# The first tile table of an attention and expert kernel: its running sum as a masked product and one sum, its parts dealt over other sequences

## What is computed

```python
x = x + attention(layernorm(x), ctx, ctx)        # 16 heads of 16 features
probs = softmax(layernorm(x) @ router)           # 8 experts
weights, picks = top_k(probs, 2)                 # two experts for each token
x = x + sum_over_the_two_picks(weight * down[e](silu(h @ gating[e]) * (h @ up[e])))
```

## Time and profile before

| | |
|---|---|
| median of 3 runs | 1268.08 us |
| lowest, highest | 1267.72, 1269.12 us |
| the profiled execution | 1269.64 us, its span 1267.9 us |
| TensorE busy | 1221.0 us (96% of the span) |
| VectorE busy | 646.1 us (51%) |
| ScalarE busy | 562.0 us (44%) |
| POOL busy | 423.9 us (33%) |
| mean granted TensorE clock | 0.993 of full |
| stage A | 0 to about 533 us |
| expert stage | about 533 us to the end |

### The profile page before, as it was taken

How to read it: one execution, slowest core, us unless ns; L and a number is a source line. 1 busy time by engine, 2 the same in 40 slices (tenths; PEclk the granted TensorE clock), 3 DMA queues, 4 the chain that set the end, 5 groups by cost and what they waited for, 6 DMA issues and landing times.

```text
span 1267.9 us, 30811 instructions
## 1 busy us (share of the span) xinstructions
PE 1221.0 (96%) x11246; PEld 994.7 (78%) x11247; DVE 646.1 (51%) x1762; ACT 562.0 (44%) x926; POOL 423.9 (33%) x354
## 2 busy tenths in 40 slices
PE   7999999999999999689999999999999999999996
PEld 5677677777767766578887888888888888888996
DVE  3778787888888878623453333222222222332332
ACT  4566666666666665525322222222222222222442
POOL 4112333333333333322563222333332322222322
PEclk9999999999999999889999999999999999999999
DMA  5444444455544432414444333333333333333432
GB/s 150 135 118 127 148 148 147 152 151 154 151 138 151 122 114 82 113 38 68 80 90 68 52 52 51 53 50 50 51 52 50 52 53 51 50 51 42 54 51 32
DMA packets 171586, 112.45 MB, mean 89 GB/s; under 512 B 103344, under 2 KB 158640, under 8 KB 171472
## 3 DMA queue, kind: packets, MB, share of 16 engines
q1 hardware_dynamic: 143984, 72.75, 23.5%
q0 software_dynamic: 26400, 37.09, 16.8%
q10 hardware_dynamic: 1088, 1.05, 0.2%
HBM read 48.59 MB, written 45.46 MB: 74 GB/s over the span
## 4 chain that ended last, share of the span: by engine, by line
PE 87%; DVE 5%; DMA 2%; issue 2%; another core or an unknown queue 2%; ACT 1%; SPq 0%; POOL 0%; ACTq 0%; POOLq 0%; DVEq 0%
PE banks L527 69%; PE banks L556 5%; PE banks L570 5%; PE banks L581 4%; DVE row_max L1064 1%; PE banks L562 1%; PE banks L533 1%; DMA heads<-qT 1%; PE banks L597 1%; DMA out<-x_sb,token 1%; PE banks L605 1%; DVE att_rows L1077 1%; DVE q_less L1071 1%; DMA x_sb<-in_x 0%
## 5 line engine op out<-in xcount | busy, mean ns | idle before, releaser
L486 POOL DMA_INDIRECT out<-x_sb,token x135 | 210.3, 1558 | 477.1 <-DVE x_sb L1386 409.9
L895 ACT ACTIVATE qT<-banks 128x1024 f32<-128x1024 f32 (+1 forms) x75 | 70.3, 938 | 473.7 <-PE banks L527 412.5
L1380 DVE TENSOR_TENSOR heads<-qT,banks 128x1024 f32<-128x1024 f32 (+1 forms) x75 | 83.5, 1114 | 355.8 <-PE banks L527 340.2
L527 PE MATMUL banks<-xnT,probs 128*128 128x256 f32 (+1 forms) x1184 | 242.5, 362 | 4.8 <-issue 4.8
L527 PE MATMUL banks<-down_sb,heads 128*128 x1080 | 245.5, 379 | 1.6 <-DVE x_sb L1386 0.9
L527 PE MATMUL banks<-xnT,kT 128*128 128x256 f32 (+1 forms) x1216 | 242.9, 357 | 3.6 <-ACT probs L889 3.6
L527 PEld LDWEIGHTS banks<-xnT,probs 128*128 128x128 f32 x1184 | 209.2, 191 | 33.2 <-issue 7.7
L527 PEld LDWEIGHTS banks<-xnT,kT 128*128 128x128 f32 x1216 | 211.7, 190 | 29.4 <-issue 4.3
L527 PEld LDWEIGHTS banks<-down_sb,heads 128*128 128x128 f32 x1080 | 204.0, 190 | 29.2 <-issue 2.2
L439 POOL DMA_INDIRECT sorted_x<-xn,slots_now x128 | 124.9, 976 | 251.1 <-PE banks L556 140.9
L1064 DVE TENSOR_REDUCE row_max<-banks 128x16 f32<-128x2048 f32 x64 | 146.6, 2291 | 58.6 <-PE banks L556 58.4
(11 more groups left out here) (168 smaller groups left out, 1293.0 us busy)
## 6 DMA issues: line engine op xcount, KB each, us to landing
xn<-sorted_x SPq DMA_DIRECT2D x240, 64.0 KB
x_sb<-in_x SPq DMA_DIRECT2D x16, 512.0 KB, 3.9
ctxT_sb<-in_ctx SPq DMA_DIRECT2D x16, 512.0 KB
heads<-kT SPq DMA_DIRECT2D x128, 64.0 KB
heads<-qT SPq DMA_DIRECT2D x128, 64.0 KB
out<-x SPq DMA_DIRECT2D x16, 512.0 KB
gate_sb<-_L_ffn_kernel_gating_EDF SPq DMA_DIRECT2D x8, 512.0 KB
up_sb<-in_L_ffn_kernel_up_EDF SPq DMA_DIRECT2D x8, 512.0 KB
```

The costliest lines, as they stand in the source:

```text
L486: pool.indirect_dma_start(out=out[:, :], out_offset=bass.IndirectOffsetOnAxis(ap=token[:, v, h:h + 1], axis=0), in_=ys[:, 2 * u + h, :], i ...
L527: last = nc.tensor.matmul(dst, lhsT, rhs, start=(i == 0), stop=(i == len(pairs) - 1))
L895: nc.scalar.activation(gatedT[:, 0:w * F], gate_up[:, 0:w * F], ACT.Silu).then_inc(s_silu, 1)
L1380: nc.vector.tensor_tensor(fusedT[:, u, 0:w * F], gatedT[:, 0:w * F], gate_up[:, 1024:1024 + w * F], ALU.mult).then_inc(s_fuse, 1)
```

## The change

The running sum over the experts becomes a product of `n_pairs` with a constant mask of 8 by 8 ones and zeroes (`up_to`, one where the second expert is not after the first) and one sum over the last axis. POOL makes the mask once, near its start. Every `add_up_tiles` of the early and the late table uses this form. The notes `done_to` and `done` move from the early table to the start of part 1 of the late table. The early table's parts are dealt anew: the counting and the running sum behind sequence 59, the expert of each tile and the tiles skipped behind sequence 60, the writing of the tables behind sequence 61. Step counts change with it (24 to 15 for the early table).

```diff
+        up_to = sb("up_to", [P, EXPERTS, EXPERTS])
...
-        EARLY_STEPS = 24
+        EARLY_STEPS = 15
         PADS_MADE = EARLY_STEPS + 3
-        PAIR_STEPS = EARLY_STEPS + 32
-        TABLE_STEPS = PAIR_STEPS + 24
+        PAIR_STEPS = EARLY_STEPS + 29
+        TABLE_STEPS = PAIR_STEPS + 18
...
             root(1)
+            nc.gpsimd.memset(up_to[:], 1.0).then_inc(s_up_to, 1)
+            pool.wait_ge(s_up_to, 1)
+            nc.gpsimd.affine_select(out=up_to[:], in_=up_to[:], compare_op=ALU.is_ge, fill=0.0, base=0,
+                                    pattern=[[1, EXPERTS], [-1, EXPERTS]], channel_multiplier=0).then_inc(s_up_to, 1)
             for i in range(SPARE_TILES):
                 pool.dma_start(sorted_x[SPARE + i * P:SPARE + (i + 1) * P, :], blank[:]).then_inc(s_blank, 16)
...
-            def add_up_tiles(steps, experts):
-                if experts[0] == 1:
-                    steps.then(nc.vector.tensor_copy(tiles_to[:], n_pairs[:]))
-                for e in experts:
-                    steps.then(nc.vector.tensor_tensor(tiles_to[:, e:e + 1], tiles_to[:, e - 1:e], n_pairs[:, e:e + 1], ALU.add))
+            def add_up_tiles(steps, room):
+                part = room[:, 0:EXPERTS * EXPERTS].rearrange("p (a b) -> p a b", b=EXPERTS)
+                steps.then(nc.vector.tensor_tensor(part, n_pairs[:].unsqueeze(1).broadcast_to([P, EXPERTS, EXPERTS]), up_to[:],
+                                                   ALU.mult))
+                steps.then(nc.vector.reduce_sum(tiles_to[:], part, AX.X))
...
                 if part == 1:
                     tile_starts_passed(steps, over)
                     steps.then(nc.vector.reduce_sum(n_pairs[:], over[:, :, 0:m:2], AX.X))
+                    add_up_tiles(steps, early_rooms[1])
                 if part == 2:
-                    add_up_tiles(steps, range(1, 5))
+                    experts_of_tiles(steps, past, EARLY)
+                    tiles_skipped(steps, past, past_tiles, n_pairs, EARLY)
                 if part == 3:
-                    add_up_tiles(steps, range(5, EXPERTS))
-                    steps.then(nc.vector.tensor_scalar(done_to[:], tiles_to[:], float(EARLY), None, ALU.min))
-                    steps.then(nc.vector.tensor_tensor(done[:, 1:EXPERTS], done_to[:, 1:EXPERTS], done_to[:, 0:EXPERTS - 1],
-                                                       ALU.subtract))
-                    steps.then(nc.vector.tensor_copy(done[:, 0:1], done_to[:, 0:1]))
-                if part == 4:
-                    experts_of_tiles(steps, past, EARLY)
-                if part == 5:
-                    tiles_skipped(steps, past, past_tiles, n_pairs, EARLY)
                     write_table(steps, 0, EARLY, 2 * P)
...
             def late_table(part):
...
                 if part == 1:
                     steps = Steps(dve, s_table, EARLY_STEPS, 6)
+                    steps.then(nc.vector.tensor_scalar(done_to[:], tiles_to[:], float(EARLY), None, ALU.min))
+                    steps.then(nc.vector.tensor_tensor(done[:, 1:EXPERTS], done_to[:, 1:EXPERTS], done_to[:, 0:EXPERTS - 1],
+                                                       ALU.subtract))
+                    steps.then(nc.vector.tensor_copy(done[:, 0:1], done_to[:, 0:1]))
                     steps.then(nc.vector.tensor_tensor(n_pairs[:], n_pairs[:], done[:, 0:EXPERTS], ALU.subtract))
-                    add_up_tiles(steps, range(1, EXPERTS))
+                    add_up_tiles(steps, late_rooms[1])
...
                 if part == 3:
-                    add_up_tiles(steps, range(1, EXPERTS))
+                    add_up_tiles(steps, late_rooms[1])
...
                     if b == 3 and g == EARLY_GROUPS + 2:
                         early_table(1)
+                    if b == 0 and g == EARLY_GROUPS + 3:
                         early_table(2)
+                    if b == 1 and g == EARLY_GROUPS + 3:
                         early_table(3)
-                    if b == 0 and g == EARLY_GROUPS + 3:
-                        early_table(4)
-                    if b == 1 and g == EARLY_GROUPS + 3:
-                        early_table(5)
```

More of the change, by code:

```diff
@@ L198, in moe_attention @@
         s_qh = [sem("query_heads_spread_0"), sem("query_heads_spread_1")]
-        s_res, s_blank, s_pad = (sem(n) for n in ("resid_stored", "blanks_written", "pads_written"))
+        s_res, s_blank, s_pad, s_up_to = (sem(n) for n in ("resid_stored", "blanks_written", "pads_written", "prefix_mask_ready"))
         s_rows_out = [sem(f"rows_written_room{r}") for r in range(ROOMS)]
@@ L1213, in early_table @@
                     steps.then(nc.vector.reduce_sum(n_pairs[:], over[:, :, 0:m:2], AX.X))
+                    add_up_tiles(steps, early_rooms[1])
                 if part == 2:
-                    steps = Steps(dve, s_table, 0, 3)
-                    add_up_tiles(steps, range(1, 5))
+                    steps = Steps(dve, s_table, 0, 5)
+                    experts_of_tiles(steps, past, EARLY)
+                    tiles_skipped(steps, past, past_tiles, n_pairs, EARLY)
                 if part == 3:
-                    steps = Steps(dve, s_table, 0, 8)
-                    add_up_tiles(steps, range(5, EXPERTS))
-                    steps.then(nc.vector.tensor_scalar(done_to[:], tiles_to[:], float(EARLY), None, ALU.min))
-                    steps.then(nc.vector.tensor_tensor(done[:, 1:EXPERTS], done_to[:, 1:EXPERTS], done_to[:, 0:EXPERTS - 1],
-                                                       ALU.subtract))
-                    steps.then(nc.vector.tensor_copy(done[:, 0:1], done_to[:, 0:1]))
-                if part == 4:
-                    steps = Steps(dve, s_table, 0, 14)
-                    experts_of_tiles(steps, past, EARLY)
-                if part == 5:
-                    steps = Steps(dve, s_table, 0, 16)
-                    tiles_skipped(steps, past, past_tiles, n_pairs, EARLY)
+                    steps = Steps(dve, s_table, 0, 10)
                     write_table(steps, 0, EARLY, 2 * P)
@@ L1258, in late_table @@
                 if part == 2:
-                    steps = Steps(dve, s_table, EARLY_STEPS, 20)
+                    steps = Steps(dve, s_table, EARLY_STEPS, 17)
                     experts_of_tiles(steps, past, LATE)
@@ L1273, in late_table @@
                     past, past_tiles, over = table_room(late_rooms, SINGLES)
-                    steps = Steps(dve, s_table, PAIR_STEPS, 12)
+                    steps = Steps(dve, s_table, PAIR_STEPS, 6)
                     experts_of_tiles(steps, past, SINGLES)
```

## The result

The changed kernel took 1265.16 us in the median of 6 runs (1262.54 to 1267.68), the kernel before 1269.26 us in the median of 6 (1267.72 to 1270.0). The ratio is 0.9967, with a 95% interval of 0.9952 to 0.9981: 4.1 us faster, and clear of no change. The profiled execution took 1262.54 us, with a span of 1260.8.

A forecast was written before the change was run, and what follows sets the result against it. TensorE was taken as the bound, except where it waited for VectorE's row maxima of sequences 60 and 62. Terms -1.64 + 0.46 - 0.86 = -2.04 us gave 1266.0 us from the 1268.08 median; range 1263.0 to 1268.9.

The forecast's parts named there:

- the likeliest case: Whole kernel: the measured time would lie within 0.2% (2.5 us) of no change; chance 0.52.
- Part 1: Behind sequence 59: shorter sum and moved notes free VectorE 1.68 us earlier; TensorE's idle time limits the gain to -1.64 us.
- Part 2: Behind sequence 60: the `tiles_skipped` steps arrive, delaying the maximum of 61 up to 0.86 us; +0.46 us shows.
- Part 3: Behind sequence 61: the `tiles_skipped` steps leave the path to the maximum of 62; all counts, -0.86 us.
- rival A: The forecast itself: all three terms, both half-clock stretches (518 to 526, 546 to 554) as before; 1266.0 us, chance 0.50.
- the sign of A: In the granted-clock windows after the change, two stretches below 1.0 would show that the forecast's own case held.
- Rival B: Less idle time keeps TensorE's clock up: first stretch gone, -3.9 us, 1264.2; second too, 1262.4; chance 0.24.
- Rival C: Gain given back at VectorE's wait before 545.23, if that ends by a clock of its own; 1268.1 us, chance 0.14.
- the unnamed wait: VectorE's 12.45 us wait before the last attention's turning at 545.23, for something the profile does not name.
- Rival D: Slower: 0.46 us more TensorE waiting behind sequence 60 brings the clock down there; 1269.4 us, chance 0.12.
- third stretch: Another half-clock stretch, behind sequence 60, like that of 518 to 526 (8 us at 0.57), costing 3.4 us.
- The covers: Late table hidden beside TensorE's products, POOL's mask work hidden by waits behind it; both cost zero.

The follow-up runs named there:

- busy_before60: The kernel before with idle TensorE products, 7 ahead of the turning of sequence 60's maxima and 5 behind; table work unchanged; 1267.43 us, 0.9980 of the kernel before.
- before_again: The kernel before once more, no edit, for a second profile; 1270.77 us, 1.0005 of the kernel before.
- dose8: The changed kernel with eight small VectorE copies added at the end of the early table's part behind sequence 59; 1269.33 us, 0.9993 of the kernel before.
- sum_only: The kernel before with only the early table's running sum replaced, mask on POOL, notes and dealing kept; 1247.73 us, 0.9988 of the kernel before.
- after_third: The changed kernel once more, no edit, as the mark for kernels beside it; 1266.71 us, 0.9970 of the kernel before.
- after_again: The changed kernel once more, no edit, on the chip where the kernel before took 1249.87 us; 1245.43 us, 0.9964 of it.
- busy: The changed kernel with idle products filling TensorE's remaining waits, from behind sequence 60 to behind the first expert tile's up products; 1263.76 us, 0.9947 of the kernel before.

## Why the prediction was right or wrong

The median fell within the range, at 1265.16 for 1266.0. But the gain was 4.1 us, where the forecast had 2.0, and the likeliest case, a change too small to measure, was not the one that came. That the median itself came so near is in part luck: the forecast started from 1268.08, the median of three runs of the kernel before, and six have 1269.26. By the ratio it had forecast 0.9984, and 0.9967 was measured. The part on VectorE's work was right; the clock was not.

- **Part 1, -1.64.** Measured 1.68 at the maximum of 60 in three profiles (9.88 to 8.20). The pair took 0.51 us, as the shapes had said (0.52). Right.
- **Part 2, +0.46.** The maximum of 61 came 0.82 us later relative to that of 60 and its turning 0.42, as forecast (506.88 - 496.80 = 10.08, for 508.98 - 499.32 = 9.66). But the loss ended there. Before, the taking off of the maxima waited until 509.96, 10.64 us behind the maximum of 60; after, it came at 507.43, 10.63 behind. It waits for the turned logits, 0.98 us behind the turning before and 0.55 after. The term was mis-sized: nothing for 0.46. POOL's row writes may be why, as at the end of stage A, but no run tried it. Before, a write ran from 508.21 to 509.17, across the turning at 508.98; in busy_before60 one ran across it too, and the taking off came 1.00 us behind. After, the write was over at 506.66, ahead of the turning at 506.88, as in before_again and dose8, where the taking off came 0.50 and 0.58 us behind.
- **Part 3, -0.86.** From the taking off (507.43, or 509.96 before) to the maximum of 62: 6.07 before, 5.36 after, so 0.71. Nearly right. The three terms are -2.40 in all for -2.04.
- **The clock.** The step that failed is rival A's "both half-clock stretches as before", with the two stretches read off one profile. The kernel before pays for one more than the changed kernel: behind sequence 60, at 2.16 us, in before_again, or, in the profile that the prediction was built on, in the first expert products, at 2.7 us. Of the six profiles in which TensorE waited for the maximum of 60, five had the fall behind it; of the eight in which it did not wait or was kept busy, none. The fall's price is not one number: from 60 to 61 it was 2.16 us in before_again, 1.35 in dose8 and 1.03 in sum_only, against profiles with the same work there and no fall. The changed kernel still shows two stretches, which the prediction had as the sign of A, but its second is in the last gate products (6.27 us at 530.57), inside VectorE's wait, where it does not show. To the second expert unit the two kernels differ by 5.6 us (68.70 and 68.74, for 62.99 and 63.17): 2.4 of work, 2.2 to 2.7 of the one stretch, 0.5 of the shorter one ahead of the maximum of 63, and smaller pieces. That the medians have 4.1 and 3.9 is not fully accounted for; falls further on, as in after_third, are some of it. That filling the wait alone gave 2.5 us shows that the clock has a part.
- **Rival B** had the mechanism (less idle time, the clock stays up) and -3.9 us, with a chance of 0.24, but named the wrong stretch: that ahead of the maximum of 63 was shorter in the first profile after and full in after_again. Removing it, in busy, brought the maximum of 63 1.49 us nearer to that of 62, for the 1.87 at most that B had. In weighing its chance it counted the 0.86 us less idle time ahead of the turning of 62, and not the 1.64 us gone ahead of that of 60, where the clock also fell. busy_before60 gained 2.5 us by activity alone. The Trainium skill, page "TensorE: Matmul & The Clock Gate", section "Part 1: The HAM clock gate", holds that the throttled state is the default and that activity releases it; that run agrees.
- **Rival C** did not come: the unnamed wait ended at 541.38 in place of 545.23 and lasted 12.50 us for 12.45, so it moved along. The reason given against it held: the eight row writes began at 529.99 in place of 533.88, and the wait ended behind them both times.
- **Rival D** did not come either; 0.82 us more on VectorE behind 60 took no clock down. Its third stretch behind 60 exists, but in the kernel before, and it cost 2.16 us there, where D had put 3.4 on it.
- **The covers** of the late table and the mask held.

## What to carry to other kernels

When the bottleneck engine is TensorE and it waits for another engine in a tight stage, a microsecond taken off that wait can be worth more than one (here 2.4 us of work went with a gain of about 4), since it can also keep the clock up; look at where the granted clock falls in several executions, not in one, before sizing it. And test it cheaply: fill the wait with products whose result nobody reads. If the kernel gets faster, the clock was part of the price.

## What had not been expected of the hardware

- In sum_only the clock fell after 0.55 us and 1.47 us of idle time with only the turning between them. In the changed kernel, with the 1.47 us alone in that place, it did not.
- The stretches at half clock move from one execution of a kernel to the next, and two executions can take the same time with different ones (1269.64 and 1269.82 us).
- POOL's row writes, eight back to back, held up a signal that VectorE awaited from TensorE: released at 542.35 with them for a product that ended at 538.68, at 538.05 without. On the chip of after_again the wait ahead of the last attention's turning was 4.33 us, and not 12.5. The writes were in place and ran from 527.04 to 536.86, and VectorE went on at 530.26, among them; why is open.
- The same kernel took 1249.9 us on one chip and 1270 on two others.
